# GpSimd makes both normalisations' deviations of an iteration in one pair of two-column instructions

## What is computed

```python
u  = cond(x)                                  # diffusion along both axes and a logistic term
hn = layernorm(u, ln1_w, ln1_b)               # mean, variance, 1/sqrt(var + 1e-5)
q, k, v = split(hn @ in_proj_w.T + in_proj_b) # 16 heads of 16 features
x1 = u + (causal_softmax(q k) v) @ out_proj_w.T + out_proj_b
h2 = layernorm(x1, ln2_w, ln2_b)
gates = top2(softmax(h2 @ router_w.T))        # 8 experts
out = x + x1 + sum over experts of gates * (gelu(h2 @ w1) @ w2)
```

## Time and profile before

| what | value |
|---|---|
| median of three runs | 716.42 us |
| span of the profiled execution, first to last instruction | 715.1 us |
| mean granted TensorE clock, share of full speed | 0.907 |
| TensorE matmul busy | 588.2 us, 82% |
| VectorE busy | 434.7 us, 61% |
| ScalarE busy | 349.2 us, 49% |
| GpSimd busy | 464.4 us, 65%, 562 instructions |
| additions of EPS, L405 | 64, 25.6 us in all, mean 401 ns |
| powers, L406 | 64, 49.5 us in all, mean 774 ns |

### The profile page before, as it was taken

How to read it: one execution, slowest core, us unless ns; L and a number is a source line. 1 busy time by engine, 2 the same in 40 slices (tenths; PEclk the granted TensorE clock), 3 DMA queues, 4 the chain that set the end, 5 groups by cost and what they waited for, 6 DMA issues and landing times. The chain is left out here.

```text
span 715.1 us, 10162 instructions
## 1 busy us (share of the span) xinstructions
PE 588.2 (82%) x2640; PEld 409.1 (57%) x2640; DVE 434.7 (61%) x1028; ACT 349.2 (49%) x814; POOL 464.4 (65%) x562
## 2 busy tenths in 40 slices
PE   2667786777679877889997899988699999999992
PEld 1334454554456645656665566666467766766761
DVE  1266689879999999655977799969735000111110
ACT  4434443334335544438674466645346555444440
POOL 5787677797697538666678865864585843434432
PEclk9779997867579989889999799999999999999997
DMA  4367864222122214313333313343344544443342
GB/s 127 125 224 225 252 162 103 62 71 48 42 64 69 46 31 86 69 42 67 68 82 66 78 23 69 68 83 54 68 91 80 119 71 73 67 68 61 69 53 22
DMA packets 51547, 59.83 MB, mean 84 GB/s; under 512 B 7386, under 2 KB 47075, under 8 KB 51428
## 3 DMA queue, kind: packets, MB, share of 16 engines
q0 software_dynamic: 18288, 23.28, 20.4%
q1 hardware_dynamic: 33204, 35.91, 17.7%
HBM read 35.89 MB, written 27.46 MB: 89 GB/s over the span
## 5 line engine op out<-in xcount | busy, mean ns | idle before, releaser
L982 PE MATMUL b_y<-w_s,hm_hmT 128*128 x568 | 138.0, 387 | 11.5 <-ACT y L551 10.8
L967 PE MATMUL b_h<-w_s,xT 128*128 x284 | 135.2, 599 | 1.6 <-ACT xT L512 1.6
L449 POOL DMA_INDIRECT out_dram<-y,xin x71 | 119.5, 1683 | 26.1 <-issue 21.9
L982 PEld LDWEIGHTS b_y<-w_s,hm_hmT 128*128 128x128 f32 x568 | 104.1, 193 | 25.8 <-issue 14.3
L1119 PE MATMUL b_at<-ident,pv_prod 128*128 128x128 f32 x544 | 79.0, 298 | 23.8 <-DVE pv_prod L913 23.8
L913 DVE TENSOR_TENSOR pv_prod<-kv,pr 128x1024 f32<-128x1024 f32 (+2 forms) x80 | 85.0, 1105 | 21.1 <-PE b_at L1119 20.9
L684 DVE TENSOR_SCALAR y<-b_y,xin,live 128x256 f32<-128x256 f32 x24 | 13.1, 544 | 137.2 <-PE b_y L982 137.2
L847 DVE TENSOR_TENSOR qk_prod<-q,kv 128x1024 f32<-128x1024 f32 (+2 forms) x80 | 89.2, 1139 | 2.6 <-ACT kv L581 1.8
L1119 PEld LDWEIGHTS b_at<-ident,pv_prod 128*128 128x128 f32 x544 | 70.2, 158 | 27.7 <-issue 22.0
L414 POOL DMA_INDIRECT xs_d<-ring,slot_row x64 | 71.2, 1112 | 18.7 <-issue 18.1
L855 DVE TENSOR_REDUCE sc<-qk_prod 128x64 f32<-128x1024 f32 (+2 forms) x80 | 82.1, 1051 | 0.3
(11 more groups left out here) (168 smaller groups left out, 1026.1 us busy)
## 6 DMA issues: line engine op xcount, KB each, us to landing
xin<-xs_d SPq DMA_DIRECT2D x71, 132.5 KB, 2.2
w_s<-in_L_ffn_w_dram SPq DMA_DIRECT2D x16, 512.0 KB, 4.2
xp<-in_x_dram SPq DMA_DIRECT2D x32, 128.0 KB
xud<-in_x_dram SPq DMA_DIRECT2D x32, 128.0 KB
out_dram<-x POOLq DMA_DIRECT2D x32, 128.0 KB, 3.2
xud<-in_x_dram SPq DMA_DIRECT2D x32, 126.0 KB
out_dram<-y,xin POOLq DMA_INDIRECT x71
xud<-in_x_dram SPq DMA_DIRECT2D x64, 1.0 KB
```

Source lines behind the costliest of these rows:

```text
L449: pool.indirect_dma_start(out_rows, bass.IndirectOffsetOnAxis(ap=xin[:, j % NX, H:H + 1].bitcast(U32), axis=0), y[:, j % NY, :], None, com ...
L967: mm = pe.matmul(b_h[:, :], xT[:, k * P:(k + 1) * P], w1_s[:, bass.ds(e * (HC * F) + k * F, F)], start=(k == 0), stop=(k == HC - 1))
L982: mm = pe.matmul(b_y[:, 0:H], hmT[:, k * P:(k + 1) * P], w2_s[:, bass.ds(e * (FC * H) + k * H, H)], start=(k == 0), stop=(k == FC - 1))
```

## The change

In each iteration, `deviations` waits for both statistics, the first normalisation's of tile g + 3 and the second's of tile g - 2, and makes both deviations in one addition and one power on two columns. Where only one of the two is due (g below 2 and above 28), a and b select one column. Statistics and deviations are laid out by the iteration that makes them, with the normalisation as the inner index, so that the two columns of an iteration lie together. One semaphore, rstd, takes the place of two. The call stands where the first deviation stood.

```diff
-        power = sb("power", [P, 1])
+        power = sb("power", [P, 2])
...
-            def deviation(g, k):
-
-                pool.wait_ge(s[("stats1", "stats2")[k]], g + 1)
-                i = g % 2
-                link(pool.tensor_scalar(rstd[:, k, i:i + 1], mv[:, k, i, 1:2], EPS, None, ALU.add))
-                pool.tensor_tensor(rstd[:, k, i:i + 1], rstd[:, k, i:i + 1], power[:, :], ALU.pow).then_inc(s[("rstd1", "rstd2")[k]], 1)
+            def deviations(g):
+
+                i, a, b = g % 2, 0 if g + 3 < G else 1, 2 if 0 <= g - 2 else 1
+                if g + 3 < G:
+                    pool.wait_ge(s["stats1"], g + 4)
+                if 0 <= g - 2:
+                    pool.wait_ge(s["stats2"], g - 1)
+                link(pool.tensor_scalar(rstd[:, i, a:b], mv[:, i, a:b, 1:2].rearrange("p k o -> p (k o)"), EPS, None, ALU.add))
+                pool.tensor_tensor(rstd[:, i, a:b], rstd[:, i, a:b], power[:, 0:b - a], ALU.pow).then_inc(s["rstd"], 1)
...
                 if g < 0 <= g + 3:
-                    deviation(g + 3, 0)
+                    deviations(g)
                 if g + AHEAD + 1 < G:
                     neighbours(g + AHEAD + 1)
-                if 0 <= g < G - 3:
-                    deviation(g + 3, 0)
+                if 0 <= g < G + 2:
+                    deviations(g)
                 if 0 <= g - 2 < G:
-                    deviation(g - 2, 1)
                     add_x1(g - 2)
...
             def unit(src, g, k):
 
-                dve.wait_ge(s[("rstd1", "rstd2")[k]], g + 1)
+                at = g + 2 * k - 3 * (1 - k)
+                dve.wait_ge(s["rstd"], at + 4)
...
-                dve.tensor_scalar(dst, src, mv[:, k, g % 2, 0:1], rstd[:, k, g % 2:g % 2 + 1], ALU.subtract,
+                dve.tensor_scalar(dst, src, mv[:, at % 2, k, 0:1], rstd[:, at % 2, k:k + 1], ALU.subtract,
                                   ALU.mult).then_inc(s[("xhat1", "xhat2")[k]], 1)
...
-                    dve.bn_aggr(mv[:, 0, (g + 3) % 2, :], small[:, 48:54]).then_inc(s["stats1"], 1)
+                    dve.bn_aggr(mv[:, g % 2, 0, :], small[:, 48:54]).then_inc(s["stats1"], 1)
...
-                        dve.bn_aggr(mv[:, 1, g % 2, :], small[:, 54:60]).then_inc(s["stats2"], 1)
+                        dve.bn_aggr(mv[:, g % 2, 1, :], small[:, 54:60]).then_inc(s["stats2"], 1)
```

More of the change, by code:

```diff
@@ L149, in adaln_moe_block @@
             w1_in w2_in
-            sums_ready scaled du_ready stats1 stats2 rstd1 rstd2 xhat1 xhat2 hT_ready hT_sb h2T_ready h2T_sb
+            sums_ready scaled du_ready stats1 stats2 rstd xhat1 xhat2 hT_ready hT_sb h2T_ready h2T_sb
             qkv_ready qk_sb v_sb sc_ready exp_ready pv_piece pv_used aT_sb o_ready x1_ready lg_ready lg_sb
@@ L443, in add_y @@
                     pool.wait_ge(y_added[(j - 1) % 2], behind)
-                    pool.tensor_tensor(passed[:, j:j + 1], power[:, :], power[:, :], ALU.add)
+                    pool.tensor_tensor(passed[:, j:j + 1], power[:, 0:1], power[:, 0:1], ALU.add)
                 elif j >= 1:
```

## The result

The changed kernel takes **712.65 us** (median of 8 runs, 710.5 to 713.59) against 716.21 us for the kernel before beside it (8 runs, 714.52 to 719.1): a ratio of 0.9947 [0.993, 0.9963]. It is faster by 3.6 us, and the forecast was 712.8 us. The sum was right, but not the terms: for three of its four no gain that lasted is shown, and the fourth gave its time in another way than the prediction said.

What follows compares the result with a forecast made beforehand. No engine is full throughout the attention steps up to 533 us, then TensorE is; gains before pass through. Terms 1.00 + 0.45 + 1.00 + 1.16 = 3.6 us, so 716.42 - 3.6 = 712.8 us; range 709.5 to 717.0.

Steps and rivals of the forecast that it cites:

- Bounds and cover: Gains before 533 us pass to the end one for one; waits for deviations from 43 to 107 us are given nothing.
- The six covered waits before 100 us: VectorE's waits for the second deviation, 43 to 107 us; shortening them only lengthens its wait for the projection: no gain.
- No cost of the joint wait and the layout: One semaphore, transposed layout and common wait, about 0.3 us for the new pair on GpSimd, delay no reader and cost nothing.
- The second column, +0.38: A second column repeats the GpSimd power's arithmetic in full, +0.38 us, so an undisturbed pair is worth 0.50 us.
- the free column: Rival: the power's second column costs nothing, so a pair is worth 0.88 us; 711.3 us, chance 0.25.
- 145 and 161 us, 1.00: VectorE waits for GpSimd's unbroken stretch; two pairs at 0.50 us add to 1.00 and stay.
- 210 us, 0.45: VectorE's 0.45 us wait for a pair slowed by its products is saved and persists.
- 380 and 398 us, 1.00: VectorE waits 3.28 and 4.73 us for GpSimd; two pairs at 0.50 us win 1.00.
- 446 us, 1.16: The new power, held by VectorE's first product alone, ends 1.16 us earlier, on the chain into the row addition behind.
- The cap of 1.25: Limit on the gain at 446 us: the row addition at 460.59 needs y written at 459.04 plus 0.30 us issue.
- Absorbed (715.4): Rival: DMA loads and expert tiles hold their pace at 380, 398, 446 us; only GpSimd's stretch to 161 pays; chance 0.20.
- The slower case by TensorE's clock: Rival: TensorE runs further passes at its lower clock, 1.69 us each; three make 717.9 us; chance 0.12.

Runs made afterwards that it cites:

- the 22 pairs off the path: Against the kernel before: one two-column pair in 22 iterations, two one-column pairs kept in the five at 145, 161, 380, 398 and 446 us; 716.2 us, 1.0005.
- all pairs apart: The changed kernel with joint wait, layout and single semaphore kept, but each deviation made by its own one-column addition and power in all 27 iterations; 717.35 us, ratio 1.0008.

## Why the prediction came out right

The time, 712.65 us, lies 0.15 from the forecast; the terms of the sum do not.

- **Bounds and cover: right.** The stage behind 533 us has TensorE busy for 150.0 us of 150, before and after, and what VectorE is ahead at 545 us, 6.4 us, is 6.1 at the end (715.1 against 709.0). The six covered waits before 100 us gave nothing that lasted (the lead at 121.9 us is 0.16), VectorE's wait for the projection grew instead (2.82 us at 66.22, from 1.62), and the 22 pairs off the path are worth 1.0005.
- **No cost of the joint wait and the layout: right** as far as 1.0008 [0.9984, 1.0032] with all pairs apart can tell.
- **The second column, +0.38: too much by 0.22.** It measured 0.155. The step that failed is "I take it that a second column repeats them in full". Of the 0.38 us by which a power exceeds an addition, 0.22 don't depend on the width. The Trainium skill, GPSIMD Engine Reference, section 3.1, makes an element of a two-input operation 2.6 cycles, beside a dispatch cost; the additions agree with it (2 ns a column), the power's 0.158 us a column does not. The true price of a pair, 0.72 us, is nearer to the free column's 0.88 than to the 0.50 taken; by the prediction's own places it would have led below 712 us.
- **145 and 161 us, 1.00: won and lost.** Alone, the two pairs won 1.37 us by 161 us; in the changed kernel the lead was 1.24 there, with 0.70 at 131 us already. The failed step is "They stay, because VectorE is the full engine of the next stage". A full engine keeps a lead only if its instructions keep their length; VectorE's products were lengthened beside GpSimd's work (4.53 for 2.94 us), and the gain was gone 35 us later.
- **210 us, 0.45: not won.** The lead at that tile is -0.91, and the pair is among the 22 that gave nothing.
- **380 and 398 us, 1.00: won (0.7, and 1.1 by these pairs alone) and given back, in the main.** The failed step is that it counted two pairs on VectorE's wait and ended there. TensorE, with 1.08 us of wait in place of 3.36, went through the matmuls behind at the lower level for longer (3.78 and 1.64 against 3.53 and 1.03 us), and then it, not VectorE, set the pace.
- **446 us, 1.16: the place was right, the mechanism wrong, and the size too small.** The step "should be held by the first product alone" failed: the power started 0.18 us ahead of that product and wasn't held. The prediction's own times say so too, as they start the power near 446.5 and the product at 446.77. The cap of 1.25 was wrong too: the second row addition of before doesn't use the y of 458.57 but an earlier one, and in the changed kernel it starts 0.02 us after the start of the y at 456.91, without waiting for it. And the prediction followed the pair only to its own end, and not to what it makes of the next instruction: the row addition's 3.70 us, not the pair's time, was the cost. The term measured 1.7 to 1.85 us where it can be followed; none of the 13 kernels shows a gain with the row addition held by both products, but the other half of the 3.6 us isn't placed.
- **The rivals.** Absorbed (715.4) had the places the wrong way round: the stretch up to 161 us, which it let pay, gave nothing that lasted, and 446 us paid. The slower case by TensorE's clock happened in small: the two groups of matmuls behind 398 us took 0.86 us more, and 0.7 had been won there.

So a sum of four terms came out right although three of them (2.45 us) show no gain that lasted, and the fourth, with 1.7 to 1.85 us for its 1.16, is half of what was measured. That is a right forecast of the sign and of the last place, and a lucky one of the size.

## What to carry to other kernels

Where two engines slow each other, a removed microsecond isn't won or lost as such: look at which instruction comes next on the shortened engine and on which side of the other engine's long instruction it starts, since 0.2 us there made 1.85 us on TensorE here. Before you sum up gains of several places, follow each to the next place where the engines meet, and ask whether it is still there; and test a place by undoing it alone and by doing all but it, because only the second showed that the pair at 446 us wasn't needed.

## What the runs showed of the hardware

- A power on GpSimd costs 0.57 us for one column and 0.158 us for each further one up to 64 (10.55 us); an addition 0.19 us and 2 ns.
- A row addition takes 1.59 us by itself (460.59). Issued 0.15 to 0.16 us after VectorE had begun a pair of two-input products it took 3.70 or 3.71 us in all five profiles that had it so; issued 0.57 to 0.80 us after the start of such a product, 1.94 to 2.16 us in all seven; and 1.63 us in the one that issued it 0.05 us ahead of a product. In all twelve held cases it ended 1.50 to 1.55 us after the end of a product: in the five of the second one, in the seven of the one that was running. A prefix scatter 0.15 us behind the products was stretched likewise, to 3.09 us from 1.00. The Trainium skill, GPSIMD Engine Reference, section 1, has the two engines share their interfaces to SBUF, in contention for VectorE's instructions with two SBUF inputs; the traces agree, with three value products at 4.53 us in place of 2.94.
- VectorE's normalisation, with one tile and two columns as inputs, took 1.10 us in the kernel before, where GpSimd's diffusion runs beside it (195.31 us), and 0.42 in the changed kernel (196.74).
